# Opening of the masked cross-attention phase: norm columns by way of DRAM, another order of the first loads and splits, and GpSimd's share of the first token tile

## What is computed

```python
xq  = layer_norm(x, qn_w, qn_b)                    # per row, then times w, plus b
ctx = layer_norm(context, cn_w, cn_b)
q = (xq @ q_w).reshape(B, N, H, D)                 # B=16, N=M=256, H=16, D=32, C=512
kv = (ctx @ kv_w).reshape(B, M, 2, H, D)
k, v = kv[:, :, 0], kv[:, :, 1]
attn = where(mask, neg, einsum('bnhd,bmhd->bhnm', q, k) * scale)
out = einsum('bhnm,bmhd->bnhd', softmax(attn), v).reshape(B, N, C)
x = x + out @ proj_w + proj_b
```

## Time and profile before

| | us |
|---|---|
| median of 3 runs | 2777.63 (2776.95 to 2779.87) |
| the profiled execution, its time | 2780.86 |
| its span, first to last instruction | 2779.2 |
| TensorE busy (98% of the span) | 2714.4 |
| VectorE busy (68%) | 1881.7 |
| ScalarE busy (56%) | 1565.4 |
| GpSimd busy (27%) | 742.2 |

### The profile page before, as it was taken

How to read it: one execution, slowest core, us unless ns; L and a number is a source line. 1 busy time by engine, 2 the same in 40 slices (tenths; PEclk the granted TensorE clock), 3 DMA queues, 4 the chain that set the end, 5 groups by cost and what they waited for, 6 DMA issues and landing times.

```text
span 2779.2 us, 68809 instructions
## 1 busy us (share of the span) xinstructions
PE 2714.4 (98%) x24256; PEld 2362.8 (85%) x24256; DVE 1881.7 (68%) x5488; ACT 1565.4 (56%) x4829; POOL 742.2 (27%) x935
## 2 busy tenths in 40 slices
PE   6999999999999999999999999999999999999997
PEld 5888888888888888888888888888888888888886
DVE  6778888887534444344487777777667777777776
ACT  5777777777211111112287777777766666666654
POOL 2333343320000000000023333333324324333333
PEclk9999999999999999999999999999999999999998
DMA  4333333242210211103121111113011101111100
GB/s 150 109 105 95 114 115 118 94 140 94 85 47 30 60 49 51 51 30 106 55 61 45 45 45 45 45 38 111 32 46 45 44 31 45 45 38 38 45 30 24
DMA packets 148214, 180.54 MB, mean 65 GB/s; under 512 B 16432, under 2 KB 77872, under 8 KB 147632
## 3 DMA queue, kind: packets, MB, share of 16 engines
q1 hardware_dynamic: 148144, 179.63, 20.3%
HBM read 122.97 MB, written 56.62 MB: 65 GB/s over the span
## 4 chain that ended last, share of the span: by engine, by line
PE 40%; DVE 5%; issue 2%; ACT 2%; POOL 1%; POOLq 0%; DVEq 0%; ACTq 0%
PE cross_work L172 15%; PE causal_work L172 7%; PE cross_probsT L1974 2%; PE cross_attended L1993 2%; PE cross_scores L1953 2%; PE cross_scores L1974 2%; PE causal_attended L1993 1%; PE causal_scores L1974 1%; PE causal_scores L1953 1%; PE causal_probsT L1974 1%; PE cross_scores L1902 1%; DVE causal_scores L1341 1%; POOL causal_y L630 1%; PE causal_probsT L1935 1%; PE cross_probsT L1935 1%
## 5 line engine op out<-in xcount | busy, mean ns | idle before, releaser
L2759 ACT ACTIVATE mlp_h<-mlp_f,mlp_b1col 128x512 f32<-128x512 f32 x128 | 88.3, 690 | 524.3 <-PE mlp_f L2963 524.3
L2963 PE MATMUL mlp_f<-mlp_xT_hi,mlp_w 128*128 128x512 f32 x1024 | 335.4, 389 | 0.0
L2981 PE MATMUL mlp_acc<-mlp_w,mlp_hT_hi 128*128 128x512 f32 x1024 | 315.2, 389 | 0.0
L2864 DVE CAST mlp_hT_hi<-mlp_h 128x512 fp32r<-128x512 f32 x128 | 58.1, 454 | 370.0 <-ACT mlp_h L2759 369.9
L817 ACT ACTIVATE mask_prob<-mask_scores,mask_low 128x256 f32<-128x256 f32 x512 | 238.3, 488 | 94.9 <-DVE mask_low L1341 94.8
L817 ACT ACTIVATE cross_prob<-cross_scores,cross_low 128x256 f32<-128x256 f32 x512 | 237.8, 500 | 7.9 <-DVE cross_low L1335 7.7
L1341 DVE CUSTOM_DVE_ANT_0 mask_scores<-mask_scores,mask_mask 128x256 f32<-128x256 f32 x512 | 198.7, 459 | 52.9 <-PE mask_scores L1953 51.7
L172 PE MATMUL causal_work<-causal_xT_hi,causal_w 128*128 128x256 f32 x1008 | 226.7, 296 | 0.4
L2963 PEld LDWEIGHTS mlp_f<-mlp_xT_hi,mlp_w 128*128 128x128 f32 x1024 | 192.1, 188 | 40.6 <-DVE mlp_xT_lo L2850 0.4
L2981 PEld LDWEIGHTS mlp_acc<-mlp_w,mlp_hT_hi 128*128 128x128 f32 x1024 | 192.2, 188 | 39.9
L817 ACT ACTIVATE causal_prob<-causal_scores,causal_low 128x128 f32<-128x128 f32 (+1 forms) x512 | 211.7, 436 | 19.3 <-DVE causal_low L1341 18.7
(11 more groups left out here) (343 smaller groups left out, 8272.4 us busy)
## 6 DMA issues: line engine op xcount, KB each, us to landing
cross_x_in<-after_attention SPq DMA_DIRECT2D x17, 512.0 KB, 3.7
mask_x_in<-in_x SPq DMA_DIRECT2D x16, 512.0 KB, 4.3
mask_c_in<-in_ctx SPq DMA_DIRECT2D x16, 512.0 KB, 5.2
mask_res<-in_x SPq DMA_DIRECT2D x16, 512.0 KB, 3.7
after_attention<-mask_res SPq DMA_DIRECT2D x16, 512.0 KB, 2.8
mlp_x<-after_attention SPq DMA_DIRECT2D x8, 1024.0 KB, 5.5
mlp_stage<-in_L_xattn_fc_w SPq DMA_DIRECT2D x8, 1024.0 KB, 5.6
after_layer<-mlp_y SPq DMA_DIRECT2D x8, 1024.0 KB, 4.3
```

Of the source, the lines that this page charges most:

```text
L2759: act.activation(h32[:, m % 2, :], F1[m % 2][:], ACT.Gelu, bias=b1col[:, m:m + 1]).then_inc(s["gelu"], 1)
L2963: ins = pe.matmul(F1[m % 2][:], W[2 * (m // 4)][:, a, k, m % 4 * P:(m % 4 + 1) * P], xT[p][:, k, :], start=(k == 0 and n == 0), stop=(k == ...
L2981: ins = pe.matmul(ACC[t][:], hT[a][:, m % 2, t * P:(t + 1) * P], W[2 * (m // 4) + 1][:, p, m % 4, :], start=(m == 0 and n == 0), stop=(m = ...
```

## The change

1. `where_vecs` now gives four transfers, one per vector. Each copies 512 single elements of 4 bytes from DRAM to a new DRAM tensor `mask_columns`, [128, 4, 4], which has the layout of `wcol`. The source pattern walks the quarter q first (4 steps), then 128 rows; the target pattern walks 128 rows, then 4 channels.
2. On SP, matrices 0 and 1 are issued right behind these four. Then SP waits until the four have landed (`vec_loaded`), issues one transfer of 128 x 64 bytes from `mask_columns` to `wcol` (signal `columns_loaded`), then matrix 2, the mask, the bias and matrix 3.
3. ScalarE waits for `columns_loaded`, does `turned(0, 0)` and `turned(0, 1)` first, then `matrix_hi(0)`, `turned(0, 2)`, `turned(0, 3)`, `matrix_hi(1)`, `matrix_hi(2)`. VectorE's order follows.
4. For batch 0 the high parts of the turned rows are cast by GpSimd (`turned_hi(0, k)`), ahead of `constants()`, and no more by VectorE.

```diff
--- before.py
+++ after.py
@@ -187,6 +187,7 @@
 
     normed_at = [nc.dram_tensor(f"mask_normed_{n}", [B, S, C], F32).ap() for n in ("rows", "context")
                  ] if masked_ctx else []
+    columns = nc.dram_tensor("mask_columns", [P, 4, KC], F32).ap() if masked_ctx else None
 
     def spread(i):
         return causal or masked_ctx and i < 3
@@ -350,9 +351,8 @@
 
     def where_vecs():
         if masked_ctx:
-            return [(wcol[q * QUAD:(q + 1) * QUAD, i, :],
-                     v.rearrange("(i k) q -> i k q", i=QUAD)[:, :, q:q + 1].rearrange("i k o -> i (k o)"))
-                    for i, v in enumerate(vecs[0:4]) for q in range(QUADS)]
+            return [(columns.rearrange("(q i) v k -> v q i k", q=QUADS)[i], v.rearrange("(i k) q -> q i k", k=KC))
+                    for i, v in enumerate(vecs[0:4])]
         out = [(g_rep[:], vecs[0].partition_broadcast(P)), (b_rep[:], vecs[1].partition_broadcast(P))]
         if cross:
             out += [(f1b[:], vecs[2]), (f2b[:], vecs[3].partition_broadcast(P)),
@@ -427,8 +427,10 @@
             load_vecs()
             load_matrix(0)
             load_matrix(1)
+            sp.wait_ge(s["vec_loaded"], IT * NV)
+            sp.dma_start(wcol[:], columns).then_inc(s["columns_loaded"], IT)
+            load_matrix(2)
             load_mask(0, first=True)
-            load_matrix(2)
             sp.dma_start(p_bias[:], vecs[4].partition_broadcast(P)).then_inc(s["bias_loaded"], IT)
             load_matrix(3)
             yield OPENED
@@ -570,7 +572,7 @@
 
         def turned_hi(b, k):
 
-            if k % 2 == 0:
+            if k % 2 == 0 and not (isinstance(b, int) and b == 0):
                 pool.wait_ge(*((s["qk_ps"], KC * b) if k else (s["x_left"], b)))
             hold(pool, s["t_act"], NP * b + k + 1, s)
             pool.tensor_copy((cT if k // 2 else xT)[0][:, 2 * (k % 2):2 * (k % 2) + 2, :], t32[k // 2][:, k % 2]
@@ -728,6 +730,8 @@
             for t in range(TT):
                 pool.tensor_scalar(c_in[:, t], c_in[:, t], minus_mean[:, TT + t:TT + t + 1],
                                    rstd[:, TT + t:TT + t + 1], ALU.add, ALU.mult).then_inc(s["x_ready"], 2)
+            for k in range(NP):
+                turned_hi(0, k)
             constants()
             yield OPENED
         if causal:
@@ -748,6 +752,7 @@
             yield OPENED
         pool.wait_ge(s["vec_loaded"], IT * NV)
         if masked_ctx:
+            pool.wait_ge(s["columns_loaded"], IT)
             pool.wait_ge(s["bias_loaded"], IT)
         yield from turn(0, prev=False)
         with pool.Fori(1, B - 1) as b:
@@ -1145,13 +1150,13 @@
             for t in range(TT):
                 act.activation(x_in[:, t], x_in[:, t], ACT.Identity, scale=rstd[:, t:t + 1],
                                bias=first_bias[:, t:t + 1]).then_inc(s["first_ready"], 1)
-            matrix_hi(0)
-            act.wait_ge(s["vec_loaded"], IT * NV)
+            act.wait_ge(s["columns_loaded"], IT)
             turned(0, 0)
             turned(0, 1)
-            matrix_hi(1)
+            matrix_hi(0)
             turned(0, 2)
             turned(0, 3)
+            matrix_hi(1)
             matrix_hi(2)
             qk(0, 0)
             exps(0, 0)
@@ -1281,9 +1286,6 @@
             dst_t = (xT if k < 2 else cT)
             sl = slice(2 * (k % 2), 2 * (k % 2) + 2)
             if masked_ctx:
-                if not squares(b):
-                    dve.wait_ge(s["t_act"], NP * b + k + 1)
-                    dve.tensor_copy(dst_t[0][:, sl, :], t32[k // 2][:, k % 2]).then_inc(s["t_hi"], 1)
                 dve.wait_ge(s["t_hi"], NP * b + k + 1)
                 dve.tensor_tensor(dst_t[1][:, sl, :], t32[k // 2][:, k % 2], dst_t[0][:, sl, :].bitcast(F32),
                                   ALU.subtract).then_inc(s["t_lo"], 1)
@@ -1797,12 +1799,12 @@
         dve.sem_inc(s["proj_read"], 1)
         if masked_ctx:
             front(0)
-            matrix_lo(0)
             turned(0, 0)
             turned(0, 1)
-            matrix_lo(1)
+            matrix_lo(0)
             turned(0, 2)
             turned(0, 3)
+            matrix_lo(1)
             matrix_lo(2)
             mask_floats(0)
             qk_lo(0, 0)
```

## The result

| | before | the change |
|---|---|---|
| median of 22 runs each, us | 2776.98 (2773.98 to 2780.67) | 2781.64 (2779.11 to 2783.42) |
| ratio, 95% interval | | 1.0018 [1.0012, 1.0024] |
| the profiled execution, its time | 2780.86 | 2781.16 |

The change makes the kernel 4.7 us slower. The forecast was 3.8 us faster. Stages have to be compared, not the two spans.

What follows compares the result with a forecast made beforehand. The opening was taken to bound the kernel: ScalarE's start (17.37 us) plus 12.3 us of splitting. Starting 3.9 us earlier, less 0.1 for the chain, gave 2777.63 - 3.8 = 2773.8 us, range 2771.8 to 2783.0.

Steps and rivals of the forecast that it cites:

- Issue: SP's queue: twelve of sixteen issues go, saving 7.8 us; matrix 0 issued at about 4.4 us instead of 12.22.
- The four small transfers: DMA: 2112 packets, 132 per engine, at 15 ns each take 2.0 us (1.2 to 11.1).
- The far bound, 84 ns: Upper price per small packet, taken from packets of 2 KB; at it the change would lose 5.3 us.
- The columns' way: SP's wait ends at about 7.7 us; the columns' load queues behind matrices 0 and 1, `columns_loaded` at 13.4.
- The chain from there: Splits on ScalarE, GpSimd and VectorE from columns to values take 12.4 us, before 12.3; edit worth nothing within 0.5.
- The sum: ScalarE starts 3.9 us earlier, less 0.1 for the chain: 3.8 us won, 2773.8 us against the median.
- The values' shift is found again at the end: Test sign: TensorE's values come at 25.9 instead of 29.72 us; the forecast is wrong if the end doesn't shift alike.
- rival C: TensorE's clock falls otherwise in the slow stretches: forecast plus or minus 2.5 us; chance 0.07 beyond 1.8 us of gain.
- A: The four transfers run on only four DMA engines: 1.9 us lost at 15 ns; chance 0.34 up to 22 ns.
- B: Four DMA engines with dear DRAM writes: loss passes 5.6 us from 22 ns, 2787.3 us at 30 ns; chance 0.12.
- D: Nothing moves, because turn 0 waits for something else, such as batch 1's rows or statistics: 2777.6 us; chance 0.05.

Runs made afterwards that it cites:

- e1_long_first: The change with the four transfers walking 128 rows first instead of 4 quarters, still by DRAM, tensor laid [4, 128, 4]; 2781.76 us, 1.0019 to before.
- e4_short_first_sbuf: The change with its four transfers, same patterns, going straight into the SBUF tile, without DRAM tensor, second load or SP's wait; 2771.49 us, 0.9981 to before.
- f1_apart: The change with each of the 2048 elements written to a 64-byte place of its own in DRAM; 2782.72 us, 1.0023 to before.
- g1_one_piece: `f3_one_dram` with its DRAM vector copied as one 2 KB piece and spread into single elements on the way into SBUF; 2775.51 us, 0.9999 to before.
- f3_one_dram: The change with three vectors going straight into SBUF and only the last by DRAM, 512 single elements; 2785.56 us, 1.0023 to before.

## Why the prediction was wrong, point by point

- *Issue.* Wrong: twelve issues went, but the four that stayed took 9.2 us, and matrix 0 was issued 6.7 us later than forecast. A transfer's issue on SP took 0.66 us for 128 elements; for 512 I took the same. That is right with 128 rows first (0.63 in `e1_long_first`), but with 4 quarters first it is 1.33 even into SBUF, and 3.25 for the one behind the rows. So `e4_short_first_sbuf` issues matrix 0 at 8.65: 4.3 of the 6.7 us are this, and it wins all the same.
- *The four small transfers.* **This is the step that failed.** I took 15 ns a packet and 2.0 us in all; the wait was over 9.6 us later than that gave. The form of the term was wrong as well as its size: I multiplied a number of packets by a price, and the packets' own times were not even dear (8.4 ns each in the change). The runs show a delay outside them that grows far less than their number. From the first packets bound for DRAM (5.3, 5.3, 8.4, 9.8 and 10.9 us in the DMA views, to within 0.5) to the end of the wait it is 12.0 us for 2048 writes, 13.3 and 10.9 for 1024 (first or last in the queue), 9.7 for 512 and 6.5 for 128: not twice the delay for sixteen times the writes. The far bound, 84 ns, gave 5.3 us lost, near the 4.7 measured. That is luck of size, not the same mechanism: at 84 ns the engines would have been busy, and in the change they were idle. The sentence on the Trainium skill that stood beside this step ("DMA: Bandwidth & Descriptors", Specifications: below 512 B the engine reads, modifies and writes) leaned to the right side. The trace agrees in direction only: writes of 4 bytes to DRAM were slow, but those into SBUF cost at most 10.3 ns, and 64 bytes between the elements (`f1_apart`) changed nothing. Whether reading and writing back is what takes the time, no run here shows.
- *The columns' way.* The last part was right: the load lands 0.2 behind matrix 1 (0.24 forecast).
- *The chain from there.* 13.4 us from `x_turned` to the values instead of 12.4. GpSimd's casts take 0.61 alone, but 0.90 and 0.97 beside VectorE (0.59 forecast), and VectorE's splits of matrices 0 and 1 take 2.90 and 2.88 beside GpSimd's work, where matrix 2 takes 2.48. The second of them runs beside GpSimd's `constants`, which the casts push from 10.7 us to 30.5; I had only asked whether they would be late for GpSimd itself. Under late columns the new order and casts cost 3.2 us against the old together (36.93 and 33.74), more than this 1.0, since the old order has matrix 0 split before the columns come. I costed both edits as if the columns were early.
- *The sum.* 9.6 us (wait) and 0.5 (a longer flight) and 1.0 (chain) are 11.1; 25.9 forecast for the values and 36.93 measured.
- *The values' shift is found again at the end.* In part. 7.2 us at the values, 6.2 at 1925 us, 4.7 in the medians. The first 0.7 is lost by 73 us, and in that stretch the change has the full clock where the kernel before had 0.51 and 0.66. So rival C's mechanism is there and the size is within its forecast, though no run separates it. What makes up the last 1.5 us is open; the lower mean clocks in the executions of the kernel before may be part of it. Over the fourteen other runs the median moved as far as the values to within 3.4 us, always with the same sign, except for `g1_one_piece` (0.7 later, 0.3 faster).
- *The rivals.* A is right as to the dealing and wrong as to its cost. B named the place and the sign, with the wrong price law. At its threshold (22 ns) it gave a loss of 5.6 us; the measured 4.7 stays below the 0.2% that I counted as slower. D is excluded.

## What to carry to other kernels

Don't scatter single elements of 4 bytes into DRAM, not even 128 of them: scatter on the way into SBUF, and if data must pass through DRAM write it in longer pieces (packets of 128 bytes did no harm here). When an unknown cost is bounded by rows of another kind of target, ask whether the cost is per packet at all; a fixed delay isn't found between two prices per packet. Issue first what is long to work on and needs nothing (here two matrices, 2 x 2.5 us of VectorE's splitting) and let the small transfers be issued beside that work.

## What the runs showed of the hardware that I had not expected

- A few single elements written to DRAM hold up what stands behind them for 6 to 13 us. Further small packets come in bursts with pauses in which no engine has one, and packets of 8 KB occupy their engines for 5.6 us instead of 0.32 (in `f3_one_dram`). It took as long for 512 writes as for 2048 to within 2.3 us, on four engines as on sixteen (12.0 and 11.5), and with elements adjacent or 64 bytes apart (12.0 and 11.0). 16 writes of 128 bytes and 512 of 2 KB had no such delay. Whether it is a time for completing such writes or something they block in the memory was not tried, nor sizes between 4 and 128 bytes.
- An issue on SP can be held up by what is ahead: the issue of matrix 0 took 0.59 us before, 2.65 with the change, 5.01 behind two vectors bound for DRAM; that of matrix 2 took 5.75 in `g1_one_piece`, where no single elements went to DRAM.
- GpSimd and VectorE slow each other here: a cast on GpSimd takes 0.61 us alone and up to 0.97 beside VectorE, a split on VectorE 2.5 us alone and 2.9 beside GpSimd, be it casts or `constants` (in `e4_short_first_sbuf` 2.50 with GpSimd idle, 2.88 beside `constants`).
